# Three scattered results under way instead of two, in the expert tiles of a routed block

## The reference, cut to what matters

```
x = x + xattn(layernorm(x), ctx, ctx, mask)        # 16 heads, x is 16 x 128 x 128
x = x + ffn(layernorm(x))

def ffn(h):                                        # h: 2048 tokens x 128
    probs = softmax(h @ wg.T)                      # 8 experts
    topk_w, topk_idx = top_k(probs, 2)
    topk_w = topk_w / sum(topk_w)
    h1, h3 = einsum('th,eih->tei', h, w1), einsum('th,eih->tei', h, w3)
    y = einsum('tei,ehi->teh', silu(h1) * h3, w2)
    return einsum('te,teh->th', expert_w, y)       # two experts a token
```

## Time and profile before

| what | us |
|---|---|
| three runs: 287.49, 288.73, 289.48; their median | 288.73 |
| span of the profiled execution | 289.2 |
| busy PE, DVE, ACT, POOL in it | 220.1, 214.5, 131.9, 109.8 |
| `ys<-big` of line 1048: 39 scatters, busy | 38.1 |

### The profile page before, as it was taken

The page is one execution under the profiler, slowest core; times in us unless marked ns, Lnnn a source line. Parts: engine busy times, 40 slices in busy tenths (PEclk is TensorE's granted clock), DMA queues, the critical chain, the costliest instruction groups (busy, mean ns, idle before and its releaser), DMA issues.

```text
span 289.2 us, 5289 instructions
## 1 busy us (share of the span) xinstructions
PE 220.1 (76%) x1445; PEld 161.4 (56%) x1445; DVE 214.5 (74%) x619; ACT 131.9 (46%) x291; POOL 109.8 (38%) x120
## 2 busy tenths in 40 slices
PE   0787779998989988887667674688787789997620
PEld 0663456666757665665336542477566668886410
DVE  4779966688759867895977786568895568775596
ACT  5777127554665448342145546243334435453300
POOL 4310350121403070105486556104556565555530
PEclk9996579999999999979756799589899999999855
DMA  6954411353033302331602110421342232211807
GB/s 216 318 233 118 131 35 28 92 125 86 9 98 96 94 0 67 87 100 47 207 9 67 46 39 29 99 47 30 77 79 76 82 84 73 80 52 26 236 5 217
DMA packets 38108, 26.33 MB, mean 91 GB/s; under 512 B 4748, under 2 KB 35726, under 8 KB 37696
## 3 DMA queue, kind: packets, MB, share of 16 engines
q1 hardware_dynamic: 34848, 19.76, 25.5%
q0 software_dynamic: 2656, 5.40, 6.1%
q10 hardware_dynamic: 576, 0.83, 0.9%
HBM read 12.32 MB, written 6.31 MB: 64 GB/s over the span
## 4 chain that ended last, share of the span: by engine, by line
PE 42%; DVE 30%; issue 10%; SPq 8%; DMA 4%; ACT 2%; POOL 1%; another core or an unknown queue 1%; DVEq 0%; ACTq 0%; POOLq 0%
SPq L427 8%; PE bank L528 8%; DVE m_neg L1411 6%; PE bank L759 4%; PE bank L760 3%; PE bank L733 3%; PE bank L652 3%; DMA bd<-st 3%; PE bank L746 3%; PE bank L736 3%; PE bank L693 2%; PE bank L676 2%; PE bank L734 2%; PE bank L679 2%; PE bank L534 2%
## 5 line engine op out<-in xcount | busy, mean ns | idle before, releaser
L1411 DVE TENSOR_REDUCE m_neg<-bank 128x4 f32<-128x512 f32 x64 | 43.5, 684 | 15.4 <-PE bank L693 15.0
L1048 POOL DMA_INDIRECT ys<-big x39 | 38.1, 976 | 40.0 <-DVE big L1447 19.2
L923 ACT ACTIVATE big<-bank 128x512 f32<-128x512 f32 x64 | 37.4, 597 | 20.9 <-PE bank L679 20.0
L797 ACT ACTIVATE st<-bank 128x128 fp32r<-128x128 f32 (+1 forms) x78 | 22.6, 330 | 31.6 <-PE bank L746 16.1
L1004 POOL DMA_INDIRECT xg<-rows,rows_i x24 | 24.6, 1027 | 31.8 <-DVE rows_i L1218 11.6
L693 PE MATMUL bank<-bd,st 128*128 128x512 f32 x64 | 31.1, 509 | 4.7 <-DMA bd<-st 3.8
L676 PE MATMUL bank<-m_bd,ones_b 128*128 128x512 f32 x64 | 31.3, 489 | 2.1 <-ACT big L923 1.9
L759 PE MATMUL bank<-bd,st 128*128 x78 | 24.3, 332 | 9.8 <-DVE big L1447 6.2
L1355 DVE SCALAR_TENSOR_TENSOR st<-st_hi,cst,bank 128x512 fp32r<-128x512 f32 x32 | 23.3, 747 | 11.3 <-ACT st_hi L797 9.0
L1026 POOL TENSOR_TENSOR m_bd<-mT,cst 128x512 fp32r<-128x512 f32 x16 | 17.3, 1110 | 30.1 <-DVE mT L1334 30.0
L679 PE MATMUL bank<-bd,st 128*128 128x512 f32 x64 | 27.1, 423 | 0.0
(11 more groups left out here) (174 smaller groups left out, 514.0 us busy)
## 6 DMA issues: line engine op xcount, KB each, us to landing
bd<-st SPq DMA_DIRECT2D x126, 64.0 KB, 2.0
big<-xg SPq DMA_DIRECT2D x39, 64.5 KB
raw<-in_L_ffn_w SPq DMA_DIRECT2D x2, 1024.0 KB, 9.3
raw<-ys SPq DMA_DIRECT2D x6, 256.0 KB
x_all<-in_x SPq DMA_DIRECT2D x4, 256.0 KB, 4.5
rows<-in_mask_BxS_if POOLq DMA_DIRECT2D x4, 256.0 KB, 5.2
ctx_all<-in_L_ffn_w SPq DMA_DIRECT2D x1, 1024.0 KB
ctx_all<-in_ctx SPq DMA_DIRECT2D x3, 256.0 KB, 5.2
```

Of the source, the lines that this page charges most:

```text
L923: nc.scalar.activation(prob[n % 2][:, NJ * g:NJ * (g + 1), :].rearrange("p h q -> p (h q)"), s2[k % 2][:, :], ACT.Exp, scale=SCALE).then_i ...
L1048: pool.indirect_dma_start(ys, bass.IndirectOffsetOnAxis(xt[n % XR][:, D:RW].bitcast(I32), 0), y_sb[n % YR], None, bounds_check=PAIRS - 1, ...
L1411: nc.vector.tensor_reduce(m_neg[:, H * (b - 1) + NJ * g:H * (b - 1) + NJ * (g + 1)], s1[k % s1_ring(u)][:, :].rearrange("p (j q) -> p j q" ...
```

## The change

In GpSimd's loop over the tiles, scatter n waits for the landing of scatter n - 3, not n - 2, for n = 3 to 32. From n = 33 on it is n - 4 before and after. `send`, which has a limit of two of its own, stays.

```diff
@@ -1042,7 +1042,7 @@
             for n in range(NT):
                 pool.wait_ge(ysb_ready, n + 1)
                 pool.wait_ge(in_t[n % XR], 16 * (n // XR + 1))
-                back = 2 if n < NT - 6 else 4
+                back = 3 if n < NT - 6 else 4
                 if n >= back:
                     pool.wait_ge(ysb_out[(n - back) % YR], 16 * ((n - back) // YR + 1))
                 pool.indirect_dma_start(ys, bass.IndirectOffsetOnAxis(xt[n % XR][:, D:RW].bitcast(I32), 0), y_sb[n % YR], None,
```

## The result

The changed kernel takes 278.23 us (median of 5 runs, 276.06 to 278.99) against 288.73 us: ratio 0.9635, 95% interval 0.9596 to 0.9674, some 10.5 us faster. I had forecast no change, 288.7 us, with a range from 286.2 to 291.2. The profiled execution after has a span of 274.2 us; its run took 276.06, so 1.9 us of a run lie outside its span. It is the fastest of the five: the other four have spans of 276.2 to 277.2 us.

What follows compares the result with a forecast made beforehand. The prediction took TensorE's tile work up to reduction 38, then an unbroken run of gathers and the outputs, as the bound. All terms summed to 0, leaving the 289.2 us span, 288.7 us on the runs' scale; range 286.2 to 291.2.

Steps and rivals of the forecast that it cites:

- The limit binds: GpSimd's scatters: it sat idle 30 times, 17.2 us in all, before a scatter, with two under way.
- Tile loads have slack: Load of tile n + 15 waits for a scatter's landing; the tightest, tile 17, has 1.85 to 2.55 us of slack.
- four terms that the sum puts at 0: Scatter period, tile loads, reads of results and the end of the kernel: each claimed to bring 0 us.
- Rival 1: Scatter queue: landings come no faster and the 1.6 us period stays; 288.7 us on the runs' scale, chance 0.12.
- rival 3: Slower: the six reads lie under more tile work, +1.7 to +4.0 us, taken as 291.8 us; chance 0.14.
- Their customer stands after reduction 36, at 274.64, and cannot use it: 0: Six reads released by scatter 30 go out 3.7 us earlier, but gather 0 on VectorE gains 0 us.
- The 0 at the end: After reduction 38, an unbroken run of gathers, then outputs; the last reads bring no wait, so 0 us.
- that for scatters 33 to 38: Last scatters on GpSimd: they had a limit of four already and follow their reductions, so 0 us.
- 3.5 us of the tiles' time unexplained: Reductions 31 to 35 take 3.5 us more than four tiles of 1.74 us; the row does not tie it to reads.
- So lag is gone by tile 15: GpSimd's scatters at 1.28 us each catch up with the reductions by tile 15, at 233.5 instead of 237.12 us.
- The forecast's scale: The profiled span of 289.2 us was set 0.45 us above the runs' median of 288.73, giving 288.7 us.
- Of the rivals, 2: Faster: the excess of tiles 31 to 35 goes or shrinks, gaining 1.7 to 3.5 us, taken as 286.6 us; chance 0.14.

Runs made afterwards that it cites:

- all4: Limit of four scatters under way for every scatter, against the kernel before: 278.88 us, ratio 0.961.
- after_again: The changed kernel repeated without an edit, on another chip, against the kernel before: 279.27 us, ratio 0.960 (0.9539 to 0.9669).
- again: The kernel before repeated without an edit, for a second profile: 289.50 us, ratio 0.9988 (0.9943 to 1.0033).
- slow2: Limit of two kept, the first product of each tile done twice on TensorE, against the kernel before: 291.18 us, ratio 1.0018.
- gather_late: Limit of two kept, gathers of batches 0 to 2 moved behind reduction 38, against the kernel before: 288.69 us, ratio 0.9936.
- late3: Limit of two for tiles 2 to 16 and three for 17 to 32, against the kernel before: 285.06 us, ratio 0.9837.
- one: Limit of one scatter under way for tiles 1 to 32, against the kernel before: 332.36 us, ratio 1.146.

## Why the prediction was wrong

**What was right.** The limit binds, and with three under way scatters go 1.28 us apart (1.33 in the mean, with gaps as at scatter 16, 2.29 us). Tile loads have slack: line 720 waited for none between tile 17 and the end after the change. Of the four terms that the sum puts at 0, the tile loads did cost nothing. Rival 1 is gone, since landings kept up with three under way. So is rival 3: all4, with most under way, is no slower, and in after_again the reads go out 10.1 us earlier than in again (256.9 against 267.0) over undisturbed tiles of 1.4 to 1.7 us.

**The step that failed** is "Their customer stands after reduction 36, at 274.64, and cannot use it: 0". Gather 0 and, behind it, reductions 37 and 38 can use an earlier read by up to 6.6 us (again). The 0 at the end and that for scatters 33 to 38 fail with it: in again scatter 38 starts 3.2 us behind its reduction, not 1.2, and gather 12 waits another 1.6 us. Between again and after_again, on two chips, the spans differ by 9.8 us: 6.6 at gather 0, 1.6 at gather 12, and 1.2 up to reduction 36 (263.26 against 262.02), 9.4 together.

**Why the row said otherwise.** In the first profile reduction 36 came 10 us later than in again (273.5 against 263.3), because results of TensorE reached the others up to 2.8 us after their recorded end, which is a modelled one. The eight gaps before reductions 10, 13, 15 to 17 and 32 to 34 sum to 23.5 us there and to 13.2 in again. These are the worst case, the last of the first products of a tile and ScalarE's silu of it:

```profile
266.32 0.28 PE L736 MATMUL bank<-st 128*128 x1
...
269.43 0.39 ACT L961 ACTIVATE big<-bank 128x256 f32<-128x256 f32 x1 [1.19 <-remote]
```

That covered the reads' lateness and left the time as it was. It was not the clock: the granted clock is 1.00 from 213 to 265 us in both profiles, and reduction 8 stands at 216 us in both. slow2 goes part of this way on purpose: its tiles make reduction 36 4.4 us later than in again (267.7), at the same time. So the profile showed a kernel whose two limits were nearly level, TensorE's tiles and the chain of scatters, and I took the one that had happened to be later for the bound. Two numbers in my own rows spoke against that. The scatters from 15 to 30 came (264.28 - 237.12) / 15 = 1.81 us apart, not the 1.56 of the first eleven which I carried through, and the tiles 1.74, with a lag standing at 5 us: the two chains ran at one pace. And I called 3.5 us of the tiles' time unexplained and then kept it as cover. A slack that is made of unexplained time is no slack. Worked on from reduction 10 (221.37) at 1.74 us a tile, reduction 36 falls at 266.6, 6.8 us earlier than its 273.45 (at again's 1.64 at 264.0, 9.4 us earlier), and gather 0 then waits for reads that went out at 266.50: the price that I should have put beside the 0.

**The working around it.** "So lag is gone by tile 15" used the reductions of the slow tiles; it is gone at tile 30 (scatter at 250.91, reduction at 249.73). The forecast's scale was off too: the span of 289.2 belongs to a run of some 291 us (1.9 us lie outside a span), above all runs shown; I read it as 0.45 us above the median. That was a weak hint that this execution was not a usual one, for in the experiments many runs of before are as long (spans of up to 290.1 us beside again). Of the rivals, 2 had the right sign, but its gain was bounded at 3.5 us by the excess of tiles 31 to 35, and for its mechanism, tiles slowed by late scatters or reads, the runs show nothing: outside the first profile, a tile without the extra product takes 1.61 to 1.64 us from reduction 18 to 30 with limits of two to four, where it waits for no load.

**What stays open.** Why TensorE's results came late in the first profile. None of the other thirteen profiles has it to this extent, with limits of one to four (gather_late has two such waits, 1.8 us in all). The runs without a profile agree with both, so they cannot tell how often it happens. Nor is it shown why a scatter's landing differs from one execution to the next under one limit (scatter 15 in again and late3). And the 10.5 us of the result itself are divided here only by way of again and after_again, which lack that lateness.

## What to carry to other kernels

A wait that is "not on the path" is so only by the slack of the place where it joins the path, and that slack has to be made of work that is explained; where two chains run at nearly one pace, price the change for either being the later. A limit on transfers under way sets a rate, round trip over limit, to be compared with the rate at which work comes in: if it is slower, the last customer pays for the sum over all of them, here 31 scatters, however harmless each wait looks. And one profile is one execution: take a second one, or set its span beside the runs, before its slacks are believed.

## What the runs showed of the hardware

A scattering DMA of 64 KB costs GpSimd 1.28 us from start to start (0.97 us and 0.30 us). With one under way (one) the round trip is 3.1 us in the steady stretch: it lands 2.2 us after its start (median), and the next one starts 0.85 us later. With two under way it is 3.4 to 3.6 us (1.71 to 1.79 us each). Under the six reads of 256 KB a scatter took 5.4 us to land (again, scatter 33 at 269.04), which held scatter 37 back to 2.45 us behind scatter 36 even with four under way. The Trainium skill ("DMA: Bandwidth & Descriptors", Anatomy of one DMA — SWDGE (gpsimd) path) puts a DMA of this path at 2.0 us plus its bytes over 436 GB/s and calls most of it completion latency; by that a 64 KB scatter would take 2.15 us, as an estimate. The trace of one agrees, with 2.1 us at least and 2.2 us in the median from start to landing; what a limit of one costs is more, 3.16 us from scatter to scatter in the mean.
